# A four-layer transformer chain on one core: context parts packed in their tile, the context laid out by the host, another priority table for the last half

## The chip, the cores and the metric

One NeuronCore of one Trainium2 chip runs the whole program. The metric is the device time of one launch in microseconds (us), lower is better. The engines are TensorE (PE in the profile, with its weight loads apart as PEld), VectorE (DVE), ScalarE (ACT), GpSimd (POOL) and SyncE (SP), which here only issues DMAs (SPq).

## The reference, cut to what matters

16 sequences of 256 tokens by 256 features run through four layers. Each attends to itself, to a context of 77 rows per sequence, or both; 16 heads of 16 features.

```python
# L0: x = LN(x + self_attn(x));  x = LN(x + cross_attn(x, ctx)); x = x + FF(LN(x))      (pre-norm)
# L1: x = LN(x + self_attn(x));  x = LN(x + cross_attn(x, ctx)); x = LN(x + MoE(x))     (8 experts, top 2)
# L2: x = LN(x + self_attn(x, mask)); x = LN(x + cross_attn(x, ctx)); x = LN(x + FF(x))
# L3: x = LN(x + cross_attn(x, ctx))
scores = einsum('bhqd,bhkd->bhqk', q, k) / sqrt(16)
out    = einsum('bhqk,bhkd->bhqd', softmax(scores), v)
```

(The comments stand for the four layer functions; weights, biases and layer-norm gains are inputs. Attentions are numbered 0 to 6 in the kernel: 0, 2 and 4 are self attentions, 1, 3, 5 and 6 are cross attentions with the context.)

## The kernel before, in words

The program has three phases, each a block that all engines run through in an order fixed at build time. Phase a (from 0 to about 1425 us in the trace) takes each of the 16 sequences through layer 0 and the attentions of layer 1 and scatters its tokens by expert. Phase b (to about 1950 us) runs the experts over 39 groups of rows. Phase c, the last half (from about 1950 us to the end at 3045.8 us), gathers the experts' rows and takes each sequence through attention 4 (self, with a mask), 5 (cross), the feed-forward block `l2_ff`, and attention 6 (cross).

**One attention.** TensorE projects the query (`proj`, L714), and ScalarE, VectorE and GpSimd split each projected value into three bf16 parts: `high` (L946, ScalarE), `rest` (L1096, VectorE), `middle` (L951, ScalarE), `low` (L1369, GpSimd). The parts stand in a tile `parts_q` or `parts_k` of [128, 3 parts, 2 halves of the features, 256 tokens]. SyncE copies them by DMA (`copy`, L1430) into a stack, six blocks of 16 partitions each, six DMAs for a stack; a stack then holds [96, 16 heads, tokens], so one bf16 matmul with 96 rows does the product of the split numbers. For the context the tokens are 77: before the change a context part uses 77 of the 256 columns of each half, so every partition gives two runs of 154 bytes. TensorE then makes scores once to find the row maxima (`qm`, L736, with L865 or L869 opening the bank with the mask in self attentions), VectorE reduces them (`max`, L1106), four small VectorE steps split the maxima, TensorE turns them (`turn_shift`, L744), ScalarE copies them (`turned_shift`, L955), and SyncE puts them by DMA into three more rows of the query stack (`shift_in`, L1433). Only then can TensorE make the scores again with the maxima taken off (`km`, L756, with L869 opening the bank in attention 4), ScalarE takes the exponent (L962), and TensorE multiplies by the values (`pv`, L772). VectorE and GpSimd turn and scale the result (L1132, L1136, L1374, L1140), and the output projection (`out`, L802) follows. The feed-forward block is 32 matmuls `ff` (L820, four steps of eight) and 32 of `out` (L802). The context rows of one sequence come by `ctx_load` (L1418), 128 partitions by two runs of 308 bytes in memory; there are 32 of these loads in phase a and 32 in phase c, one for each cross attention of each sequence, and as many context stacks.

**The order of the work.** `Plan.run` is a planner in the kernel's own source. Each step has a duration `us` and a delay `lag` written by hand; the planner walks through a model of the engines and always takes the step that can start first, and of several the one with the highest urgency. The urgency of a step is its remaining way to the end of its sequence in modelled us, divided by 20 (phase a) or 28 (phase c), less the number of its sequence, plus what `ahead_of` reads from the table `AHEAD` for its stage: the entry of the stage and the entry of (stage, attention), added. The stages that matter below: "scores" holds `km` and `exp`, "ffs" `ff` and `relu`, "projs" the projections with their parts and copies, "values" the value projection, "pvs" `pv`, "shifts" the way of the maxima from VectorE to the stack. Up to seven sequences are under way at once (`LANES`). The engines then run their lists in that order and wait on semaphores; nothing is reordered on the chip. For `shift_in` the planner counts 0.76 us and a lag of 2.2 us, times 1.35 for landings in phases a and c:

```python
plan.step("sync", "shift_in", b, at, us=0.76, lag=2.2, after=[("turned_shift", b, at)], gives=["shift"], landing="shift",
over[k], land[k] = end, end + s.lag * (landing if s.landing else 1.0)
urgency = {k: way / per_sequence - self.steps[k].b + (ahead(self.steps[k]) if ahead else 0.0)
plan.run("c", 28.0, ahead_of("c"), 1.35)
```

## Time and profile before

| | us |
|---|---|
| median of 3 runs | 3065.95 (3065.38 to 3067.84) |
| the profiled execution, its own time | 3048.22 |
| its span in the profile | 3045.8 |
| TensorE busy in the span | 2830.4 (93%) |
| VectorE, ScalarE, GpSimd busy | 1681.8, 1331.7, 986.7 |
| packets moved by DMA | 393627, of them 152155 under 512 B |
| mean granted TensorE clock | 0.964 of full |

The page's chain of work that ended last lies on TensorE for 29% of the span and on DMA for 3%, all of it found in phase c (the chain ends at the start of that phase). "Busy" of TensorE is modelled from pipelined matmuls. In the views of waits a line gives the engine and line that waited, what released it, the sum in us, the number of times and the longest one.

### The profile page before, as it was taken

What the parts mean: (1) busy time and instruction counts of PE and PEld (TensorE: products, weight loads), DVE (VectorE), ACT (ScalarE), POOL (GpSimd) and SP (SyncE); (2) the same over time, 40 slices, a digit from 0 to 9 for tenths busy, and PEclk for the clock granted to TensorE, in tenths of its full rate; (3) what the DMA queues carried; (4) which work ended last, traced back from release to release, by engine and by line L of the source; (5) the groups of instructions that cost most, each with busy time, mean ns of one, the idle gap of its engine ahead of it and who ended that gap; (6) DMA issues with size and microseconds to landing.
All of it is one profiled execution on the core that took longest, in us unless ns stands there. A gap on an engine that the chain in (4) does not pass through costs nothing. (4 is left out here: it accounts for less than half of the span.)

```text
span 3045.8 us, 58500 instructions
## 1 busy us (share of the span) xinstructions
PE 2830.4 (93%) x22574; PEld 2279.3 (75%) x22574; DVE 1681.8 (55%) x4086; ACT 1331.7 (44%) x2955; POOL 986.7 (32%) x1103
## 2 busy tenths in 40 slices
PE   6989999989999989975999999889999999999996
PEld 4768888768888777754888888656777777777774
DVE  4646556776755867554110010276676766767664
ACT  2535445556455455332222222245455545555442
POOL 2313224444323444322000000252344444444343
PEclk8999999999999999986999999899999999999997
DMA  9755546585664674754767766375466555666342
GB/s 141 119 72 67 63 54 89 84 114 75 75 71 59 90 98 72 190 74 135 241 225 231 224 211 220 87 111 63 53 85 76 80 79 75 82 77 78 43 50 40
DMA packets 393627, 317.68 MB, mean 104 GB/s; under 512 B 152155, under 2 KB 377307, under 8 KB 393339
## 3 DMA queue, kind: packets, MB, share of 16 engines
q1 hardware_dynamic: 370994, 276.25, 54.6%
q0 software_dynamic: 8272, 23.73, 2.8%
q10 hardware_dynamic: 14085, 13.97, 1.7%
q8 instruction: 179, 2.93, 0.5%
q14 instruction: 97, 0.79, 0.1%
HBM read 133.54 MB, written 36.57 MB: 56 GB/s over the span
## 5 line engine op out<-in xcount | busy, mean ns | idle before, releaser
L962 ACT ACTIVATE a_prob<-a_bank 128x512 f32<-128x512 f32 (+1 forms) x640 | 332.8, 603 | 146.5 <-PE a_bank L756 142.9
L1106 DVE TENSOR_REDUCE a_maxima<-a_bank 128x2 f32<-128x512 f32 (+3 forms) x576 | 339.2, 644 | 82.7 <-PE a_bank L736 82.0
L962 ACT ACTIVATE c_prob<-c_bank 128x512 f32<-128x512 f32 (+1 forms) x512 | 266.3, 599 | 194.7 <-PE c_bank L756 194.4
L989 ACT ACTIVATE b_group_hidden<-b_bank,b_b 128x256 f32<-128x256 f32 (+1 forms) x312 | 123.3, 452 | 387.7 <-PE b_bank L820 387.7
L1106 DVE TENSOR_REDUCE c_maxima<-c_bank 128x6 f32<-128x462 f32 (+1 forms) x448 | 260.4, 635 | 45.2 <-PE c_bank L736 43.9
L865 PE MATMUL a_bank<-a_causal_b,keep_identb 128*128 128x256 bf16 (+1 forms) x768 | 243.1, 316 | 29.9 <-DMA a_qs<-a_shift 12.9
L820 PE MATMUL b_bank<-b_group_xt,b_w 128*128 128x256 f32 (+1 forms) x1248 | 261.6, 364 | 6.3 <-DVE b_group_xt L1157 6.3
L802 PE MATMUL b_bank<-b_w,b_group_hidden 128*128 128x256 f32 x1136 | 251.7, 380 | 0.9 <-ACT b_group_hidden L989 0.9
L820 PEld LDWEIGHTS b_bank<-b_group_xt,b_w 128*128 128x128 f32 x1248 | 220.6, 192 | 33.7 <-DVE b_group_xt L1157 8.3
L802 PEld LDWEIGHTS b_bank<-b_w,b_group_hidden 128*128 128x128 f32 x1136 | 215.6, 190 | 29.7 <-ACT b_group_hidden L989 1.3
L1163 DVE TENSOR_TENSOR b_group_y<-b_bank,b_b 128x512 f32<-128x512 f32 (+1 forms) x39 | 25.1, 644 | 336.1 <-PE b_bank L802 336.1
L1359 POOL TENSOR_TENSOR c_tok<-c_tok,weights_row_L_xattn_ln_g 128x512 f32<-128x512 f32 x64 | 81.2, 1268 | 192.9 <-PE c_bank L705 192.7
L756 PE MATMUL a_bank<-a_qs,a_ks 99*128 99x128 bf16 x1536 | 143.5, 222 | 0.0
L736 PE MATMUL a_bank<-a_ks,a_qs 96*128 96x128 bf16 x1536 | 142.4, 220 | 0.0
L756 PEld LDWEIGHTS a_bank<-a_qs,a_ks 99*128 99x128 bf16 x1536 | 121.6, 99 | 22.9 <-issue 1.4
L736 PEld LDWEIGHTS a_bank<-a_ks,a_qs 96*128 96x128 bf16 x1536 | 120.2, 98 | 23.6 <-issue 2.2
L1132 DVE STREAM_TRANSPOSE a_flat<-a_bank 128x512 f32<-128x512 f32 x128 | 90.0, 708 | 86.5 <-PE a_bank L772 86.0
L714 PE MATMUL a_bank<-a_xt,a_at_q 128*128 128x256 f32 x512 | 131.8, 404 | 5.7 <-ACT a_xt L935 4.4
L802 PE MATMUL a_bank<-a_at_o,a_heads 128*128 128x256 f32 x512 | 131.3, 402 | 5.6 <-DVE a_heads L1140 5.4
L1152 DVE TENSOR_TENSOR a_tok<-a_bank,a_tok 128x512 f32<-128x512 f32 x80 | 54.8, 687 | 146.3 <-PE a_bank L802 146.0
L1369 POOL TENSOR_TENSOR a_parts_q<-a_rest,a_parts_q 128x512 bf16<-128x512 f32 x64 | 74.0, 1158 | 183.0 <-ACT a_parts_q L951 183.0
L1386 POOL DMA_INDIRECT c_pair_y<-sorted_out,keep_rows x64 | 62.8, 982 | 200.7 <-issue 195.1
(255 smaller groups left out, 6224.0 us busy)
## 6 DMA issues: line engine op xcount, KB each, us to landing
b_w<-in_L_xattn_e_w SPq DMA_DIRECT2D x78, 1024.0 KB, 7.4
a_qs<-a_parts_q SPq DMA_DIRECT2D x384, 128.0 KB
c_qs<-c_parts_q SPq DMA_DIRECT2D x288, 128.0 KB
a_ks<-a_parts_k SPq DMA_DIRECT2D x192, 128.0 KB, 5.9
c_ks<-c_parts_k SPq DMA_DIRECT2D x96, 128.0 KB, 5.5
sorted_in<-a_zeros SPq DMA_DIRECT2D x8, 1024.0 KB
b_group_x<-sorted_in SPq DMA_DIRECT2D x32, 256.0 KB, 6.8
sorted_out<-b_group_y ACTq DMA_DIRECT2D x32, 256.0 KB, 4.8
```

The source lines that it names most:

```text
L714: ins = pe.matmul(bank[:, 0, m * n:(m + 1) * n], weight[:, kt, m * P:(m + 1) * P], xt[:, kt, 0:n], start=(kt == 0), stop=(kt == KT - 1))
L736: ins = pe.matmul(bank[:, 0, to:to + m], qs[0:STACK, h, q * P:(q + 1) * P], ks[0:STACK, h, kt * P:kt * P + m], start=(at in CROSS), stop=( ...
L756: ins = pe.matmul(bank[0:kn, 0, to:to + m], ks[0:STACK + NPART, h, kt * P:kt * P + kn], qs[0:STACK + NPART, h, q0:q0 + m], start=(at in CR ...
L802: ins = pe.matmul(bank[:, 0, q * D:(q + 1) * D], heads[:, kt, q * P:(q + 1) * P], weight[:, kt, :], start=(kt == 0), stop=(kt == kts - 1))
L820: ins = pe.matmul(bank[:, 0, j * n:(j + 1) * n], weight[:, kt, f * P:(f + 1) * P], xt[:, kt, 0:n], start=(kt == 0), stop=(kt == KT - 1))
L865: pe.matmul(blocks, k.identb, k.causal[:, keys_first, :].unsqueeze(1).broadcast_to([P, 4 // step, P]), start=True, stop=False)
L962: act.activation(prob[0:rows, first:first + cols], bank[0:rows, 0, 0:cols], ACT.Exp, scale=SCALE).then_inc(k.own(s), 1)
L989: ins = act.activation(hidden[:, f, 0:n], bank[:, 0, j * n:(j + 1) * n], ACT.Gelu, bias=b1[:, f:f + 1])
L1106: v.tensor_reduce(maxima[:, q:q + qn, h:h + n].rearrange("p q h -> p h q"), bank[:, 0, 0:cols].rearrange("p (j q n) -> p j q n", j=n, q=qn ...
L1132: v.transpose(flat, tile(s, "bank")[:, 0, :].rearrange("p (g b c) -> p g b c", g=2, c=32)).then_inc(k.own(s), 1)
L1359: pool.tensor_tensor(x, x, over(k.gains[at][0]), ALU.mult).then_inc(k.own(s), 1)
L1369: pool.tensor_tensor(parts[:, 2, :, 0:n], rest[:, :, 0:n], parts[:, 1, :, 0:n], ALU.subtract).then_inc(k.own(s), 1)
```

## The change

Three edits. (1) `parts_of` gives a context part a packed view of the same tile, so that a part of one partition is one run of 308 bytes (two halves of 77 bf16 values) instead of two of 154; `high`, `rest`, `middle`, `low` and `copy` use it for the context. (2) The host lays the context out as [sequence, partition, half, token], so that `ctx_load` reads one run of 616 bytes a partition instead of two of 308. (3) The table `AHEAD["c"]` is replaced by another one; durations, lags, lanes, buffers and the table for phase a stay. As the modelled durations stay too, the order of phases a and b is what it was.

```diff
--- before.py
+++ after.py
@@ -456,18 +456,16 @@
                ("outs", 2): 152.6, ("norms", 3): 74.0, ("turns", 3): -0.1, ("maxima", 3): 1.6, ("shifts", 3): 0.6,
                ("pvs", 3): 1.3, ("ends", 3): -0.8, ("outs", 3): -0.1, ("norms", "l1_2"): -0.5,
                ("turns", "l1_2"): 0.2, ("gains", "l1_2"): 1.8},
-         "c": {"enters": 2.3, "norms": 8.4, ("norms", 4): -9.6, "turns": 1.2, ("turns", 4): -0.2, "gains": 4.7,
-               ("gains", 4): 30.5, "projs": 0.7, ("projs", 4): -0.5, "values": -0.4, ("values", 4): 1.4,
-               "maxima": -0.2, "shifts": 102.7, ("shifts", 4): 20.1, "scores": 0.2, ("scores", 4): 28.6,
-               "pvs": -0.2, ("pvs", 4): 0.1, "ends": -0.1, ("ends", 4): -48.7, ("enters", 5): 2.2,
-               ("projs", 5): 67.2, ("values", 5): 15.0, "outs": -1.0, ("outs", 4): 0.4, ("norms", 5): -269.4,
-               ("turns", 5): 2.9, ("gains", 5): -88.8, ("maxima", 5): -0.3, ("shifts", 5): 86.2,
-               ("scores", 5): -0.5, ("pvs", 5): 16.5, ("ends", 5): 11.0, ("outs", 5): 9.0, ("norms", "l2_ff"): -4.7,
-               ("turns", "l2_ff"): 18.2, ("gains", "l2_ff"): 5.1, "ffs": 36.7, ("ffs", "l2_ff"): 30.1,
-               ("outs", "l2_ff"): 38.3, ("enters", 6): 1.1, ("projs", 6): 77.4, ("values", 6): 121.8,
-               ("norms", 6): 4.9, ("turns", 6): -1.6, ("gains", 6): 4.8, ("shifts", 6): 2.8, ("scores", 6): 19.9,
-               ("pvs", 6): 129.6, ("ends", 6): -12.2, ("outs", 6): 29.6, ("norms", "l3"): -8.7,
-               ("gains", "l3"): 14.4}}
+         "c": {("ends", 4): 0.8, ("ends", 5): 5.5, ("ends", 6): -1.4, "ends": -1.2, ("enters", "c"): 2.2,
+               ("enters", 6): -1.3, "enters": -0.3, ("ffs", "l2_ff"): 1.9, "ffs": -1.8, ("gains", "l2_ff"): -4.1,
+               ("gains", "l3"): -0.1, ("gains", 4): -8.4, ("gains", 6): -0.4, "gains": 3.0, ("maxima", 5): -0.2,
+               "maxima": -0.2, ("norms", "l2_ff"): 1.3, ("norms", "l3"): 5.6, ("norms", 4): -7.7,
+               ("norms", 5): -16.2, ("norms", 6): -7.2, "norms": 10.8, ("outs", "l2_ff"): 0.1, ("outs", 5): 10.6,
+               ("outs", 6): 1.1, "outs": -0.4, ("projs", 4): -1.5, ("projs", 5): 4.2, ("projs", 6): 13.9,
+               "projs": 1.8, ("pvs", 6): 50.0, "pvs": -0.2, ("scores", 4): 14.9, ("scores", 5): 9.5,
+               ("scores", 6): 2.9, "scores": 4.0, ("shifts", 4): 13.8, ("shifts", 5): 4.5, ("shifts", 6): 1.8,
+               "shifts": 17.5, ("turns", "l2_ff"): 5.3, ("turns", 4): -0.8, ("turns", 6): -1.6, "turns": 1.2,
+               ("values", 4): 1.1, ("values", 5): 6.7, ("values", 6): -0.2, "values": -0.1}}
 
 
 def ahead_of(phase):
@@ -909,6 +907,13 @@
     return qs.rearrange("p h t -> p (h t)").bitcast(F32).rearrange("p (f t) -> p f t", t=S)
 
 
+def parts_of(parts, role):
+
+    if role != "c":
+        return parts
+    return parts.rearrange("p a m t -> p (a m t)")[:, 0:NPART * KT * C].rearrange("p (a m t) -> p a m t", a=NPART, m=KT)
+
+
 def rows_of(sorted_rows, rows):
     return sorted_rows[rows, :].rearrange("(q p) d -> p q d", p=P)
 
@@ -938,7 +943,7 @@
                 ins = act.activation(xt, bank[:, 0, :].rearrange("p (k t) -> p k t", k=KT), ACT.Copy)
             ins.then_inc(k.own(s), 1)
         elif s.kind == "high":
-            bank, parts, n = tile(s, "bank"), tile(s, "parts"), C if s.part == "c" else S
+            bank, parts, n = tile(s, "bank"), parts_of(tile(s, "parts"), s.part), C if s.part == "c" else S
             bias = k.biases[at][0 if s.part == "q" else 1]
             until.wait_ge(*done("proj", b, at, s.part))
             until.wait_ge(*freed(s, "parts"))
@@ -946,7 +951,7 @@
                 ins = act.activation(parts[:, 0, m, 0:n], bank[:, 0, m * n:(m + 1) * n], ACT.Identity, bias=bias[:, m:m + 1])
             ins.then_inc(k.own(s), 1)
         elif s.kind == "middle":
-            parts, rest, n = tile(s, "parts"), tile(s, "rest"), C if s.part == "c" else S
+            parts, rest, n = parts_of(tile(s, "parts"), s.part), tile(s, "rest"), C if s.part == "c" else S
             until.wait_ge(*done("rest", b, at, s.part))
             act.activation(parts[:, 1, :, 0:n], rest[:, :, 0:n], ACT.Copy).then_inc(k.own(s), 1)
         elif s.kind == "turned_shift":
@@ -1088,7 +1093,7 @@
                 ins = v.tensor_scalar(out[:, t, :], x[:, t, :], moments[:, t, 0:1], rstd[:, 1, t:t + 1], ALU.subtract, ALU.mult)
             ins.then_inc(k.own(s), 1)
         elif s.kind == "rest":
-            bank, parts, rest, n = tile(s, "bank"), tile(s, "parts"), tile(s, "rest"), C if s.part == "c" else S
+            bank, parts, rest, n = tile(s, "bank"), parts_of(tile(s, "parts"), s.part), tile(s, "rest"), C if s.part == "c" else S
             bias = k.biases[at][0 if s.part == "q" else 1]
             until.wait_ge(*done("high", b, at, s.part))
             until.wait_ge(*freed(s, "rest"))
@@ -1364,7 +1369,7 @@
                 until.wait_ge(*done("bias_fold", -1, "bias", SHIFT_AFTER[at]))
             pool.tensor_tensor(x, x, over(k.gains[at][1]), ALU.add).then_inc(k.own(s), 1)
         elif s.kind == "low":
-            parts, rest, n = tile(s, "parts"), tile(s, "rest"), C if s.part == "c" else S
+            parts, rest, n = parts_of(tile(s, "parts"), s.part), tile(s, "rest"), C if s.part == "c" else S
             until.wait_ge(*done("middle", b, at, s.part))
             pool.tensor_tensor(parts[:, 2, :, 0:n], rest[:, :, 0:n], parts[:, 1, :, 0:n], ALU.subtract).then_inc(k.own(s), 1)
         elif s.kind == "weigh":
@@ -1415,10 +1420,10 @@
             sp.dma_start(tile(s, "x"), (k.x_in if at == "a" else k.x1)[b]).then_inc(k.own(s), 16)
         elif s.kind == "ctx_load":
             until.wait_ge(*freed(s, "ctx"))
-            sp.dma_start(tile(s, "ctx"), k.ctx_in[b]).then_inc(k.own(s), 16)
+            sp.dma_start(tile(s, "ctx").rearrange("p k t -> p (k t)"), k.ctx_in[b].rearrange("p k t -> p (k t)")).then_inc(k.own(s), 16)
         elif s.kind == "copy":
             role, part = s.part
-            parts, stack, n = tile(s, "parts"), tile(s, "stack"), C if role == "c" else S
+            parts, stack = parts_of(tile(s, "parts"), role), tile(s, "stack")
             if part == 0:
                 until.wait_ge(*done("high", b, at, role))
                 until.wait_ge(*freed(s, "stack"))
@@ -1427,7 +1432,7 @@
             else:
                 until.wait_ge(*done("low", b, at, role))
             for block in COPIES[role == "q"][part]:
-                sp.dma_start(stack[block * HD:(block + 1) * HD, :, :], parts[:, part, :, 0:n]).then_inc(k.own(s), 16)
+                sp.dma_start(stack[block * HD:(block + 1) * HD, :, :], parts[:, part, :, :]).then_inc(k.own(s), 16)
         elif s.kind == "shift_in":
             until.wait_ge(*done("turned_shift", b, at))
             sp.dma_start(tile(s, "qs")[STACK:STACK + NPART, :, :], tile(s, "shift")).then_inc(k.own(s), 16)
@@ -1597,7 +1602,7 @@
     x1 = scratch("x_moe_in", [B, S, D])
     k.x1 = x1.rearrange("b (q p) d -> b p q d", p=P)
     k.out = out.rearrange("b (q p) d -> b p q d", p=P)
-    k.ctx_in = a["ctx_t"].rearrange("(k p) (b t) -> b p k t", p=P, t=C)
+    k.ctx_in = a["ctx_t"]
     k.sorted_in, k.sorted_flat = scratch("sorted_in", [ROWS_SORTED, D]), scratch("sorted_out", [PAIRS * GROUP + SINGLES * HALF, D])
     k.expert_w1 = a["L1_xattn_e_w1"].rearrange("e (k p) n -> e p k n", p=P)
     k.expert_w2 = a["L1_xattn_e_w2"].rearrange("e (k p) n -> e p k n", p=P)
@@ -1755,7 +1760,7 @@
     turn = lambda x: np.moveaxis(x.reshape(x.shape[:-1] + (H // KT, KT, HD)), (-3, -2, -1), (-1, -3, -2)).reshape(x.shape)
     paired = lambda x: np.moveaxis(x.reshape((KT, 2, H // KT // 2, HD) + x.shape[1:]), 1, 2).reshape(x.shape)
     arrays = {"x": v["x"], "mask": v["mask_1x1xSxS_ik0"].reshape(S, S),
-              "ctx_t": v["ctx_1024"].reshape(B * C, D).T,
+              "ctx_t": v["ctx_1024"].reshape(B, C, KT, P).transpose(0, 3, 2, 1),
               "columns": np.concatenate([(turn(v[n].reshape(D)) if n in _TURNED else paired(v[n].reshape(D)) if n in _PAIRED else v[n]).reshape(-1, P)
                                          for n in _VECTORS]).T,
               "rows": np.stack([v[n] for n in ROWS]),
```

## Rows read from the trace of the kernel before

**Rows 1.** The page: busy time, then granted clock in 40 slices.
```profile
PE 2830.4 (93%) x22574; PEld 2279.3 (75%) x22574; DVE 1681.8 (55%) x4086; ACT 1331.7 (44%) x2955; POOL 986.7 (32%) x1103
...
PEclk8999999999999999986999999899999999999997
```

**Rows 2.** Stretches: bounds, length, busy of PE, PEld, DVE, ACT, POOL, clock, DMA, GB/s.
```profile
1950.00:2206.00 256.00, 231.35 (x1641) 166.10 (x1642) 164.42 (x372) 114.69 (x243) 109.55 (x118) 0.93 0.61 84
2206.00:2840.00 634.00, 616.94 (x4928) 469.60 (x4926) 437.50 (x1008) 325.83 (x713) 288.52 (x321) 1.00 0.60 77
2840.00:3045.80 205.80, 176.34 (x1349) 136.96 (x1349) 117.44 (x270) 88.54 (x199) 79.64 (x90) 0.90 0.35 47
200.00:1300.00 1100.00, 1058.47 (x9982) 872.20 (x9983) 725.20 (x1847) 556.30 (x1231) 397.29 (x439) 0.98 0.59 85
```

**Rows 3.** Waits of TensorE from 2206 to 2840 us, the whole list.
```profile
PE c_bank L869 <- DMA c_qs<-c_shift: 17.0, 10, 2.6
```

**Rows 4.** Chain of work that ended last, pieces: start, length, what.
```profile
2310.44 6.95 PE c_bank L820 x32
...
2373.85 6.95 PE c_bank L820 x32
...
2404.56 6.38 DMA c_qs<-c_shift
```

**Rows 5.** Waits of TensorE from 1950 us to the end.
```profile
PE c_bank L869 <- DMA c_qs<-c_shift: 20.9, 13, 3.5
PE c_bank L705 <- DVE c_tok L1088: 11.0, 3, 4.1
...
PE c_bank L756 <- DMA c_qs<-c_shift: 2.0, 2, 1.8
PE c_bank L714 <- DMA c_ctx_t<-in_ctx_t: 1.6, 1, 1.6
```

**Rows 6.** Waits of TensorE in the whole span, those of phase a on DMAs.
```profile
PE a_bank L865 <- DMA a_qs<-a_shift: 12.9, 6, 5.9
...
PE a_bank L865 <- DMA a_qs<-a_parts_q: 10.7, 3, 7.7
...
PE a_bank L756 <- DMA a_qs<-a_shift: 9.4, 6, 3.6
...
PE a_bank L714 <- DMA a_ctx_t<-in_ctx_t: 2.6, 3, 1.9
```

**Rows 7.** DMA in 2437 to 2445 us: queue q1 (packets, MB, share), an issue.
```profile
q1 hardware_dynamic: 1842, 0.43, 33.9%
...
c_ctx_ks<-c_parts_k SPq DMA_DIRECT2D x6, 38.5 KB
```

**Rows 8.** DMA in 2429 to 2437 us, when query copies pass: queue q1.
```profile
q1 hardware_dynamic: 1198, 1.11, 93.4%
```

**Rows 9.** Issues of L1430 by tile: ns min/median/max.
```profile
L1430 SPq DMA_DIRECT2D c_qs<-c_parts_q x288: 551/601/2058, 1974.9 to 2999.1; - x144
...
L1430 SPq DMA_DIRECT2D c_ctx_ks<-c_parts_k x192: 565/617/1870, 1960.8 to 2999.8; - x192
```

**Rows 10.** Groups by line and shape, the two context parts written whole.
```profile
L1369 POOL TENSOR_TENSOR c_parts_k<-c_rest,c_parts_k 128x154 bf16<-128x154 f32 x32 | 15.3, 478 | 38.7 <-ACT c_parts_k L951 38.7
...
L951 ACT ACTIVATE c_parts_k<-c_rest 128x154 bf16<-128x154 f32 x32 | 10.5, 329 | 7.9 <-DVE c_rest L1096 7.9
```

**Rows 11.** Order of time on SyncE's queue, 2463 to 2478 us.
```profile
2468.00 0.76 SPq L1433 DMA_DIRECT2D c_qs<-c_shift  x1
2470.24 3.16 SPq L1430 DMA_DIRECT2D c_qs<-c_parts_q  x3
2473.45 1.94 SPq L1430 DMA_DIRECT2D c_ctx_ks<-c_parts_k  x3
```

**Rows 12.** Order of time on TensorE, 2464 to 2478 us.
```profile
2470.89 1.89 PE L802 MATMUL c_bank<-c_weights_at_o,c_heads 128*128 128x256 f32 x8
2474.12 0.39 PE L869 MATMUL c_bank<-c_weights_mask_k,keep_identb 128*128 128x512 bf16 x1 [1.34 <-DMA c_qs<-c_shift]
```

## The prediction, made before the changed kernel was built or run

> **What bounds the kernel.** The page comes first: TensorE is busy 93% of the span, VectorE 55%, and the clock row shows that TensorE has full clock nearly everywhere but at the start, between the phases and at the end [rows 1]. So only work, idle time or clock of TensorE can move the time. The second view is the table of stretches, because the change touches phase c in one way (its order) and phases a and c in another (the context's bytes). In phase c TensorE's busy time in the three stretches is 231.35 + 616.94 + 176.34 = 1024.6 us of 1095.8, so 71.2 us are idle: 24.7 in the 256 us of the start, 17.1 in the 634 us of the middle, 29.5 in the last 205.8 us [rows 2]. The middle is 97.3% busy. The waits of TensorE there are one single row: 10 waits, 17.0 us together, each for `shift_in` at attention 4 [rows 3]. The chain view says how regular that is: the same feed-forward block comes every 63.4 us (2373.85 - 2310.44), and one DMA of 6.4 us stands in each period [rows 4]. A new order of work must therefore be judged by two things: how many such waits it makes, and what it does to the start and the end, where 54 us of idle time lie and the mean clock is 0.93 and 0.90 [rows 2].
>
> **The context's bytes.** The 384 context copies (four stacks of six in each of 16 sequences) go from 256 packets to 128, 64 loads likewise: 57,344 fewer packets of 393,627. What is a short packet worth? When nearly only context copies pass, 1842 packets take 0.339 x 8 us x 16 engines = 43.4 us, 24 ns each [rows 7]; when query copies pass, 1198 packets of 1 KB take 0.934 x 8 x 16 = 119.6 us, 100 ns each [rows 8]. A context copy is thus 256 x 24 / 16 = 0.38 us of all engines, less than its issue of 0.617 us [rows 9]: SyncE, not the DMA engines, paces such a stack, and the issue of a long-packet copy, 0.601 us, is hardly shorter [rows 9], so I count nothing for the issue. Between a packet price that does not depend on its bytes and one that is all bytes, the saving is 0.19 us or 0 a copy, at most 1.15 us off the queue for a stack. TensorE waits on DMAs after the start are few: the shift and query-copy waits of phase a (6 + 3 + 6 = 15 waits, 33.0 us), three on the context load (2.6 us) [rows 6], and in phase c 15 on the shift (22.9 us) and one on the load (1.6 us) [rows 5]. The ten of the middle have no context copy ahead of them: SyncE issues the shift at 2468.00, and the first context copies come at 2473.45 [rows 11]. That leaves at most 20 waits x 1.15 = 23 us and 4.2 us of load waits, if a stack stood before every one; a context stack is one in three or four, so I take a sixth of it, **-3 us**, with ends 0 and -10.
>
> What the row shows is that a packet of 154 bytes costs 24 ns where one of 1 KB costs 100 [rows 7, 8]. [...]
>
> The engines' own work on a context part (ScalarE 329 ns, GpSimd 478 ns for 128x154 [rows 10]) has the same elements; the parts now start at 154-byte steps. I cost it at nothing: VectorE is 69%, ScalarE 51%, GpSimd 46% busy in the middle of phase c [rows 2], and that idle time hides it. Were each of the 64 context splits 0.3 us slower without cover, it would be 19 us; no row shows a reason.
>
> **The order.** A change of order adds and removes no instruction, so TensorE's 1024.6 us stay but for the clock. The order only decides what stands behind which landing. The wait that exists is a mistake of the model: the planner lets a shift land 0.76 + 2.2 x 1.35 = 3.7 us after its issue, the trace has 2474.12 - 2468.00 = 6.1 us [rows 11, 12], since query and key copies still fill the DMA engines. Whatever order is planned, the 2.4 us error stays; it costs time only where `km` is the next thing on TensorE's list. That is set by the table. Before, `ffs` had 66.8 and the projections of attentions 5 and 6 had 67.9 and 78.1, over `km` with 28.8 (attention 4), -0.3 (5) and 20.1 (6): work of several us is put between a shift and its scores, above all at 5 and 6, and there the middle has no wait at all [rows 3]. Afterwards `km` has 18.9, 13.5 and 6.9, `ffs` 0.1, the projections 6.0 and 15.7. So `km` of 4 and 5 now goes as soon as the model allows, ahead of the 64 matmuls of the feed-forward block that used to cover it. I expect attention 5 to wait as attention 4 does: 1.7 us each (17.0 / 10 [rows 3]). Attention 6 and some of attention 5 keep cover from projections that happen to be ready, so I take 12 further waits of 32 cross attentions: 12 x 1.7 = **+20 us**. The ends are no further wait (or the old ones gone, -21) and all 32 of 1.7 (+54). The start and end I leave as they are.
>
> **Sum.** Against the profiled execution: 3048.2 - 3 + 20 = 3065.2 us. The median of the runs shown is 17.7 us above that execution; the parts are differences and are put on the median: 3065.95 + 17, rounded down to **3082**.
>
> **The rivals.** *Feed-forward as filler, faster.* At lowest rank the feed-forward steps of 1.73 us each (6.95 us for four [rows 4]) are what is left whenever nothing else can start; spread behind the shifts, eight of them could cover the 20.9 us of shift waits in phase c [rows 5]. For it: the waits of the middle need only 1.7 us of cover. Against it: the planner does not know that cover is needed. Price: -21 - 3 = -24: **3042**; it could reach 3025 if the start, where three layer-norm waits cost 11.0 us [rows 5], packs better as well. *Same packing.* TensorE is the bound and any order with seven sequences under way may fill it as well: only the bytes remain, **3063**. For it: phase a, under a table where the feed-forward has low rank, is 96.2% busy from 200 to 1300 us (1058.47 of 1100), 1.1 points below the middle of phase c [rows 2], and it has only 12 shift waits [rows 6]. (By that rate alone phase c would be 12 us longer, between this case and mine.) *Feed-forward pushed to the end, slower by much.* If low rank leaves the blocks of the last three or four sequences until nothing else is left, the last attentions 6 come with no cover: the end's 29.5 us of idle time doubles, and half clock (the stretch has 0.90 of full) adds some 15 (an estimate: today the stretch loses 205.8 x 0.10 = 20 us of clock): +45 - 3, **3108**. It decides if more than two such blocks start after the place of the last of today's. That the change doesn't do what it says: the packed parts surely cut packets; the order surely differs; only the share of each is open.
>
> **Chances.** Waits added (3070 to 3100): 0.34. Filler (3025 to 3058): 0.29. Same packing (3056 to 3069): 0.20. Pushed to the end (3095 to 3130): 0.17. A measurement of this kernel tells about 0.2% from no change, 6 us; so faster, below 3059.8, takes 0.29 and a quarter of the third case, 0.33 together; same takes 0.14 of the third case and the nearest edges of the first and second, 0.19; slower the rest, 0.48. Both signs hold much. The range runs from 3040 to 3112: it leaves out the lower half of the second case and a third of the last. My likeliest case alone is 3070 to 3100.
>
> **What would show it.** Right: the packets drop by about 57,000; phase a, whose order is unchanged, moves by less than 10 us; the waits of TensorE in phase c list L756 behind the shift with ten or more waits near 1.7 us; the span of phase c is some 20 us above 1095.8. Wrong: the sum of shift waits falls under 10 us (filler); or the idle time of the last 200 us grows past 45 us (pushed to the end); or phase a alone gains more than 10 us, which would mean that short packets had held up the shifts.

## The result: faster by 0.84%, where slower by 0.5% was forecast

The changed kernel takes 3043.58 us (median of 7 runs, 3040.6 to 3050.39). The kernel before, run beside it on the same chip, takes 3072.01 us (3065.38 to 3085.62, 7 runs). The ratio is **0.9916, 95% interval [0.9901, 0.9932]**. The forecast was 3082, with a range of 3040 to 3112. Its likeliest case (3070 to 3100) did not happen, and the sign was wrong.

The chips of these runs differ among themselves by nearly as much as the change is worth: the kernel before takes 3050.13 us on the one of e13 to e15 and 3069.08 on the one of e16 to e18, 0.6% more. Timed on another chip, beside a kernel before of 3052.43 us, the changed kernel (run e7 below) takes 3022.63 us: ratio 0.9903 [0.9885, 0.9922]. Spans are therefore compared within one chip, or stretch by stretch. Four single executions of the runs below took two to five times as long as the rest and are left out of the ratios.

The page of the kernel after, beside [rows 1], with the line of its packets:

```profile
PE 2832.3 (93%) x22574; PEld 2279.5 (75%) x22574; DVE 1693.0 (56%) x4086; ACT 1329.9 (44%) x2955; POOL 986.1 (32%) x1103
...
PEclk9989999999999999995999999989999999999997
...
DMA packets 336285, 317.69 MB, mean 104 GB/s; under 512 B 86620, under 2 KB 319964, under 8 KB 335996
```

The same instructions, the same megabytes, 57,342 fewer packets, as counted. The span is 3040.9 us. The profiled execution of the kernel before (3048.22 us) is none of the seven timed beside this one, of which the fastest took 3065.38, so these two profiles may come from different chips; e8 and e7 below are a pair from one chip. The table of stretches, for the places of [rows 2] shifted by 8.2 us since phase b starts that much later in this execution (phase a, to which "Where the packed parts pay" comes back, is longer here and not shorter), with all of phase c behind them, first after and then before (bounds, length, busy of PE, PEld, DVE, ACT, POOL, clock, DMA share, GB/s):

```profile
1958.20:2214.20 256.00, 228.78 (x1647) 165.63 (x1648) 172.53 (x372) 113.64 (x243) 108.48 (x116) 0.94 0.50 83
2214.20:2848.20 634.00, 628.23 (x5009) 479.59 (x5008) 458.74 (x1028) 328.06 (x722) 292.48 (x326) 1.00 0.50 78
2848.20:3040.90 192.70, 163.57 (x1264) 127.43 (x1262) 101.93 (x249) 84.13 (x189) 75.87 (x86) 0.92 0.31 50
...
1958.20:3040.90 1082.70, 1020.58 (x7916) 772.66 (x7916) 733.20 (x1647) 525.84 (x1153) 476.83 (x528) 0.97 0.47 74
```

```profile
1950.00:3045.80 1095.80, 1024.63 (x7916) 772.66 (x7916) 719.36 (x1647) 529.06 (x1153) 477.72 (x528) 0.96 0.56 73
```

Phase c holds the same 7916 matmuls and is 13.1 us shorter. TensorE's idle time fell from 71.2 to 62.1 us; the other 4.0 us are busy time, which goes with a clock of 0.97 in place of 0.96. The idle time is 27.2 us at the start (24.7 before), 5.8 in the middle (17.1) and 29.1 at the end (29.5). So the gain is the middle: the row that filled it before, ten waits for the shift [rows 3], is nearly gone. The waits of TensorE in the middle stretch of the kernel after, the whole list, and then the first of its waits in all of phase c (beside [rows 5]):

```profile
PE c_bank L742 <- DVE c_least_parts L1130: 4.3, 10, 1.4
PE c_bank L867 <- DMA c_qs<-c_shift: 1.1, 5, 0.3
PE c_bank L754 <- ACT c_prob L967: 0.2, 1, 0.2
PE c_bank L800 <- ACT c_prob L967: 0.2, 1, 0.2
```

```profile
PE c_bank L703 <- DVE c_tok L1093: 12.6, 4, 7.7
PE c_bank L800 <- DVE c_heads L1145: 10.3, 7, 3.2
PE c_bank L742 <- DVE c_least_parts L1130: 9.1, 16, 1.7
```

Where a shift is waited for, the order of time on SyncE's queue and on TensorE shows why it costs so little now (beside [rows 11, 12]; in brackets the idle time before the instruction and what ended it):

```profile
2659.03 0.75 SPq L1438 DMA_DIRECT2D c_qs<-c_shift  x1
```

```profile
2659.74 1.99 PE L800 MATMUL c_bank<-c_weights_at_o,c_heads 128*128 128x256 f32 x8
2661.57 0.60 PE L754 MATMUL c_bank<-c_qs,c_ctx_ks 99*77 99x256 bf16 x4
2662.00 0.38 PE L734 MATMUL c_bank<-c_ctx_ks,c_qs 96*128 96x77 bf16 x6
2662.22 1.97 PE L712 MATMUL c_bank<-c_xt,c_weights_at_q 128*128 128x256 f32 x8
2664.12 1.07 PE L770 MATMUL c_bank<-c_prob,c_ctx_values 77*32 77x256 f32 x16
2665.35 0.39 PE L867 MATMUL c_bank<-c_weights_mask_k,keep_identb 128*128 128x512 bf16 x1 [0.16 <-DMA c_qs<-c_shift]
```

The landing is as late as it was, 2665.35 - 2659.03 = 6.3 us (6.1 before [rows 11, 12]), but TensorE has other work nearly up to it: an output projection, scores, a query projection and a value product. It waits 0.16 us instead of 1.34. The feed-forward block is not what stands there: in the chain it still comes whole, 32 matmuls of 6.91 us at a time, every 62.3 us (2380.45 - 2318.12) where it was 63.4 [rows 4]:

```profile
2318.12 6.91 PE c_bank L818 x32
...
2380.45 6.91 PE c_bank L818 x32
...
2442.80 6.91 PE c_bank L818 x32
```

### The profile page after: what moved, and what is told of

Its sections match the earlier page's. It is cut to its first block and busy times, and to the rows that moved or that the text cites. A ratio compares the mean times of both kernels' runs of the same rounds, so it can differ in the third digit from the quotient of the medians.

```text
span 3040.9 us, 58523 instructions
## 1 busy us (share of the span) xinstructions
PE 2832.3 (93%) x22574; PEld 2279.5 (75%) x22574; DVE 1693.0 (56%) x4086; ACT 1329.9 (44%) x2955; POOL 986.1 (32%) x1103
## 5 line engine op out<-in xcount | busy, mean ns | idle before, releaser
L1111 DVE TENSOR_REDUCE c_maxima<-c_bank 128x6 f32<-128x462 f32 (+2 forms) x448 | 262.9, 633 | 39.5 <-PE c_bank L734 39.2
L800 PE MATMUL a_bank<-a_at_o,a_heads 128*128 128x256 f32 x512 | 135.0, 410 | 5.6 <-DVE a_heads L1145 5.5
```

The lines of the kernel that those rows point to most:

```text
L800: ins = pe.matmul(bank[:, 0, q * D:(q + 1) * D], heads[:, kt, q * P:(q + 1) * P], weight[:, kt, :], start=(kt == 0), stop=(kt == kts - 1))
L1111: v.tensor_reduce(maxima[:, q:q + qn, h:h + n].rearrange("p q h -> p h q"), bank[:, 0, 0:cols].rearrange("p (j q n) -> p j q n", j=n, q=qn ...
```

## The experiments

Lengths of stages: a is from the start to the first transposition of phase b, b is 526.1 us long in both kernels, c is the rest. Ratios are to the kernel before on the same chip, with 95% intervals.

| run | what it is | ratio | a | c |
|---|---|---|---|---|
| e8 | kernel before again | 0.9989 [0.9973, 1.0006] | 1434.4 | 1091.9 |
| e7 | kernel after again | 0.9903 [0.9885, 0.9922] | 1417.5 | 1077.8 |
| e1 | packed parts, host-laid context, old table | 0.9927 [0.9911, 0.9942] | 1426.6 | 1088.7 |
| e2 | new table alone | 0.9961 [0.9947, 0.9975] | 1428.7 | 1082.3 |
| e3 | packed parts alone | 0.9942 [0.9927, 0.9956] | 1418.0 | 1084.5 |
| e4 | host-laid context alone | 0.9994 [0.9984, 1.0005] | 1429.5 | 1092.3 |
| e5 | packed parts in phase a alone | 0.9966 [0.9953, 0.998] | 1420.1 | 1092.3 |
| e6 | packed parts in attentions 5 and 6 alone | 0.9979 [0.9967, 0.9991] | 1425.5 | 1086.3 |
| e9 | parts at steps of 78 columns, packets as before | 0.9996 [0.9985, 1.0007] | 1426.1 | 1093.8 |
| e10 | kernel before, planned lag of phase c's shifts 4.0 for 2.2 | 1.057 [1.0546, 1.0594] | 1427.2 | 1270.2 |
| e11 | kernel after, the same | 1.0272 [1.0253, 1.0291] | 1423.4 | 1190.0 |
| e12 | kernel after, 4.0 in phase a too | 1.0546 [1.0526, 1.0565] | 1497.0 | 1188.0 |
| e13 | kernel before, shift issued by ScalarE | 0.9977 [0.9967, 0.9988] | 1426.3 | 1091.0 |
| e14 | e1, shift issued by ScalarE | 0.9934 [0.9915, 0.9952] | 1415.9 | 1077.4 |
| e15 | kernel after, shift issued by ScalarE | 0.9961 [0.9945, 0.9976] | 1420.8 | 1091.0 |
| e16 | kernel before, ten shifts covered by hand | 1.0008 [0.9993, 1.0022] | 1441.5 | 1099.2 |
| e17 | e1, ten shifts covered by hand | 0.9963 [0.9949, 0.9976] | 1431.4 | 1089.8 |
| e18 | kernel before, the same work moved to behind the scores | 1.0031 [1.0017, 1.0045] | 1443.5 | 1104.3 |

### The parts of the change, one at a time (e1 to e4, e7, e8)

e1 has every hunk of the diff but the table; e2 has the table alone. e3 has the packed parts without the host's layout, e4 that layout alone, which is these three edits:

```diff
-            sp.dma_start(tile(s, "ctx"), k.ctx_in[b]).then_inc(k.own(s), 16)
+            sp.dma_start(tile(s, "ctx").rearrange("p k t -> p (k t)"), k.ctx_in[b].rearrange("p k t -> p (k t)")).then_inc(k.own(s), 16)
...
-    k.ctx_in = a["ctx_t"].rearrange("(k p) (b t) -> b p k t", p=P, t=C)
+    k.ctx_in = a["ctx_t"]
...
-              "ctx_t": v["ctx_1024"].reshape(B * C, D).T,
+              "ctx_t": v["ctx_1024"].reshape(B, C, KT, P).transpose(0, 3, 2, 1),
```

> The packed context parts and the host-laid context, with the table for the last half that the kernel before has. Theory O (the order did it: it removes the waits on the shift in phase c): within 0.15% of the kernel before, ratio 0.9985 to 1.0; the wait row of L867 behind the shift stays near 17 to 21 us and the feed-forward block still comes every 63.4 us. Theory B (the bytes did it: short packets had held up the shifts and copies): ratio 0.991 to 0.994, the shift waits under 8 us, a period near 62.3 us. The packets drop by 57,344 under both.

> The other table for the last half, with the layout that the kernel before has. Theory O: ratio 0.991 to 0.993, period of the feed-forward block near 62.3 us, shift waits of phase c under 5 us. Theory B: ratio 0.997 to 1.0, since the new order alone only moves the waits. A third theory, that the two need each other (the new order's cover is just long enough with fewer packets): both single edits give less than a third of 0.84%.

> Only the packed context parts: 49,152 packets fewer, the context loads and the table as before. Theory O: ratio 0.9985 to 1.0005. Theory B: nearly all of what the layout gives, 0.992 to 0.995, because 384 of the 448 transfers that are shortened are these copies.

> Only the context laid out by the host: 8,192 packets fewer, the parts and the table as before. Theory O and theory B: ratio 0.999 to 1.001; the TensorE waits on the context load (2.6 and 1.6 us) may halve. More than 0.2% either way would say that HBM reads of 308 bytes cost far more than their 8,192 packets.

Measured: the layout is worth 0.73%, the table 0.39%; their sum, 1.12%, is 0.15 more than both together in e7, within what the intervals leave open. Of the layout, the packed parts are 0.58% and the host's part nothing that can be told from zero. The layout of the parts is thus the larger half of the gain, about 18 us, and not the 3 of the prediction. It does not come by the waits on the shift in phase c, as the second theory had it: they are 23.0 us in e1, where under 8 was expected. The table gains where +20 us was forecast, less than its own theory had (0.991 to 0.993). In phase c TensorE's waits on the shift come to 4.1 us, against 25.9 in e8:

```profile
PE c_bank L742 <- DVE c_least_parts L1123: 8.7, 15, 1.7
PE c_bank L754 <- DMA c_qs<-c_shift: 4.1, 7, 1.2
```

```profile
PE c_bank L756 <- DMA c_qs<-c_shift: 25.9, 13, 3.8
```

The first fence is e2, the second e8, both waits of TensorE in phase c. Here too the least parts take a piece back: 8.7 us where e8 has 2.8.

> The changed kernel once more, beside the others on one chip. If the two parts add, 0.9927 x 0.9961 = 0.989 (3018 us where the kernel before has 3051). If they share one source (both shorten the wait on the shift in phase c), 0.991 to 0.993.

> The kernel before, word for word, for a trace from this chip: ratio 0.9985 to 1.0015, the start of phase b between 1425 and 1440 us, the sum of TensorE's waits on the shift in phase c 20 to 26 us.

Both repeat what the first pair gave, and give each stage on one chip: phase a 1434.4 against 1417.5 us, phase c 1091.9 against 1077.8.

### Where the packed parts pay (e5, e6)

Both are e3 with the packed view in some attentions only:

```diff
+def parts_of(parts, role, at):
+    if role != "c":
+        return parts
+    if at not in (1, 3):          # e6: (5, 6)
+        return parts[:, :, :, 0:C]
...
```

> The context parts are packed in phase a alone (attentions 1 and 3); phase c, the loads and the table as before. Packing in both phases gave 0.9942. If the gain is spread as the copies are (half of the 384 in each phase), this gives 0.9965 to 0.998 and the start of phase b comes 5 to 10 us earlier than in the kernel before. If only phase c gains (its regular wait on the shift shrinks), this gives 0.999 to 1.001. If only phase a gains, 0.993 to 0.996.

> The context parts are packed in phase c alone (attentions 5 and 6). Spread: 0.9965 to 0.998. Only phase c: 0.993 to 0.996, with less idle time of TensorE between 2206 and 2840 us than 17 us. Only phase a: 0.999 to 1.001, start of phase b as in the kernel before.

Each shortens its own phase and leaves the other. Phase a is 1429.5 us long in the mean of e8, e4, e2 and e6, which have its parts unpacked, and 1420.6 in that of e1, e3, e5 and e7. Lengths scatter with the clock (1434.4 us at 0.95 of full in e8, 1425.5 at 0.96 in e6); TensorE's idle time in it does so less: 134.5 to 135.5 us in the former, 124.1 to 127.2 in the latter. Other executions show less of this. The kernel after of the first pair has 137.1 us of idle time in a phase a of 1436.4, beside 135.0 and 1428.3 in the kernel before. Of e16 to e18, whose hand edits touch phase c alone and which ran on another chip, e16 and e18 have 137.5 and 137.7 us, and e17, with packed parts, 134.6; the ratio of e17 to e16 is 0.9955, where e1 has 0.9927. The gain in phase a thus shows in the time of e5 (0.9966); in the idle time it is 7 to 11 us on the chips of e1 to e8 and 3 on that of e16 to e18, and the first pair, perhaps of two chips, shows none. Phase c is 5.6 us shorter in e6 and 7.4 in e3 than in e8, but 3.2 in e1, of which the slowest of its six executions was profiled (3043.63 us, median 3030.63). No single wait carries it. Phase a of e8, then of e7, in the table of stretches:

```profile
0.00:1434.40 1434.40, 1298.88 (x12129) 1059.03 (x12129) 904.35 (x2348) 678.36 (x1489) 491.63 (x548) 0.95 0.60 88
```

```profile
0.00:1417.50 1417.50, 1293.43 (x12129) 1053.43 (x12129) 903.95 (x2348) 678.32 (x1489) 491.20 (x548) 0.95 0.58 89
```

Idle time is 135.5 against 124.1 us. Some waits of TensorE in those stretches, e8 first (rows left out between them changed less):

```profile
PE a_bank L756 <- DMA a_qs<-a_shift: 9.2, 6, 3.6
...
PE a_bank L865 <- DMA a_qs<-a_parts_q: 8.1, 2, 7.9
...
PE a_bank L865 <- DVE a_maxima L1106: 6.0, 5, 3.4
...
PE a_bank L714 <- DMA a_ctx_t<-in_ctx_t: 3.2, 2, 2.9
```

```profile
PE a_bank L754 <- DMA a_qs<-a_shift: 7.6, 4, 3.4
...
PE a_bank L863 <- DMA a_qs<-a_parts_q: 6.9, 2, 6.6
...
PE a_bank L863 <- DVE a_maxima L1111: 3.1, 5, 1.0
...
PE a_bank L712 <- DMA a_ctx_t<-in_ctx_t: 1.7, 2, 1.4
```

Each gives one to three microseconds, together 7.2 of the 11.4. That the packed parts shorten just these is not shown: in the first pair the same four come to 27.5 us before and 26.7 after. What does land earlier is, first, the context copy itself: the median context copy of phase a takes 3.4 us from its issue to its landing in e8 and 2.6 in e7 (the page's DMA issues; the last column):

```profile
a_ctx_ks<-a_parts_k SPq DMA_DIRECT2D x192, 38.5 KB, 3.4
```

```profile
a_ctx_ks<-a_parts_k SPq DMA_DIRECT2D x192, 38.5 KB, 2.6
```

The context load does so too in e3, where it is not changed itself: 4.5 us against 5.8 in phase a, 2.7 against 3.9 in phase c. The key copies don't (5.8 and 5.9 us in phase a, 5.5 in both in phase c), nor do the shifts for which TensorE waits in phase c (6.4 us in both). So some transfers beside the packed ones gain and some do not; by which of them the time reaches TensorE stays open.

### Is it the number of packets, or the place of the bytes? (e9)

```diff
-    return parts...[:, 0:NPART * KT * C].rearrange("p (a m t) -> p a m t", a=NPART, m=KT)
+    return parts...[:, 0:NPART * KT * (C + 1)].rearrange("p (a m t) -> p a m t", a=NPART, m=KT)[:, :, :, 0:C]
```

e3 with one column left free behind each run of 77: the parts stand as close as in e3, but the two halves no longer touch.

> The context parts lie nearly packed: the second half begins after 78 columns, not 77, so a copy keeps its 256 packets of 154 bytes, while everything else (where ScalarE, VectorE and GpSimd write, how far apart the runs lie) is as in the packed kernel, with the table and loads of before. If the number of packets is what counts: ratio 0.9985 to 1.001, the context copy's median time to landing stays near 3.4 us, the start of phase b near 1430 us. If the engines or the density count: 0.993 to 0.996, as with packed parts, and 1418 us.

Nothing that can be told from zero is left of e3's 0.58% (idle time of phase a: 132.4 us, 2 to 3 less than in the other four): 393,627 packets as in the kernel before, a ratio of 0.9996, and 3.5 us to the landing. So the gain is the count of packets (or, which this cannot part, the length of each run), and neither where the parts lie nor what the engines do to them. What the packets cost is seen in e4 and e1, one chip and the packed parts as the only difference, from q1's share of 16 engines' time over the span: 54.0% of 3047.9 us in e4, 51.2% of 3041.4 in e1.

```profile
q1 hardware_dynamic: 362802, 276.25, 54.0%
```

```profile
q1 hardware_dynamic: 313650, 276.25, 51.2%
```

That is 26,334 - 24,915 = 1419 us of engine time for 49,152 packets fewer, 29 ns each. The trace holds the size and time of every packet and says where it comes from. 98,304 packets of 154 bytes took 24.0 ns in the mean in e4, 49,152 of 308 bytes took 31.9 in e1: a pair becomes a third cheaper, 796 us in all, 0.13 us of all engines for a copy. Most of the rest, 505 us, is the 206,848 packets of 1 KB, whose mean went from 100.2 to 97.8 ns though nothing about them was changed.

### Is the table's gain the cover of the shift? (e10 to e18)

The planner lets a shift land 3.7 us after its issue; one at attention 4 took 6.1 [rows 11, 12]. e10 to e12 let the planner count 6.2 for every shift:

```diff
-    plan.step("sync", "shift_in", b, at, us=0.76, lag=2.2, ...
+    plan.step("sync", "shift_in", b, at, us=0.76, lag=4.0 if at in (4, 5, 6) else 2.2, ...
```

(These are the shifts of phase c; e12 has 4.0 everywhere.)

> The kernel before with one number of the planner put right in phase c: the lag of the shift's landing 4.0 instead of 2.2, so that it counts 0.76 + 4.0 x 1.35 = 6.2 us as the trace shows. If the new table's gain is that it covers this landing, this order loses most of the 19 to 21 us of shift waits too: ratio 0.995 to 0.998 and waits on the shift in phase c under 8 us. If cover is not what matters, or another wait takes its place: 0.999 or above.

> The changed kernel with the same lag of 4.0 in phase c. It has 2.3 us of shift waits left in the middle, so there is little to take: 0.989 to 0.992 against the kernel before (the changed kernel alone 0.990). Above 0.994 would say that the table fits only the lags it was made with.

> The changed kernel with the lag of 4.0 in phases a and c. Phase a still waits 20.6 us on the shift in 11 places; if the planner covers half of them the ratio is 0.986 to 0.989 and phase b starts near 1410 us. If its table was fitted to the lag of 2.2, phase a gets longer and the ratio is above 0.992.

All three are 3 to 6% slower (e12 has 80 us more in phase a than e7, 1497.0 against 1417.5). In e10 the waits on the shift do fall, from 25.9 to 6.6 us, but others rise far more. The first of its waits in phase c:

```profile
PE c_bank L744 <- DVE c_least_parts L1125: 41.0, 15, 5.7
PE c_bank L705 <- DVE c_tok L1088: 26.5, 12, 4.5
PE c_bank L802 <- DVE c_heads L1140: 25.1, 12, 4.5
PE c_bank L736 <- DMA c_qs<-c_parts_q: 14.6, 9, 4.1
```

These runs say nothing on cover. Nor had they made the model truer. The trace holds the semaphore increments of each DMA, four for a shift; put to the issues in their order, they give its landing. In e8, 34 of the 48 shifts of phase c land within 3.7 us (median 2.9). In the middle stretch the ten of attention 4 take 5.7 to 8.2 us, and the twenty of attentions 5 and 6 take 2.7 to 3.0. The one at attention 4 stands behind twelve copies of 128 KB, issued in the 10 us before it (from 2400.16 us on for the shift at 2410.31). So the planner's 3.7 us were wrong for one attention in three, and e10 to e12 made them wrong for the other two. A lag of 4.0 at attention 4 alone was not tried, so that a table's ranks hold only for the durations they were found with is not shown.

e13 to e15 leave the order alone and send the shift over ScalarE's queue, where no query or key copy stands in front of it:

```diff
+            shift_in = k.plan.steps["shift_in", b, at, 0]
+            until.wait_ge(*done("turned_shift", b, at))
+            act.dma_start(tile(shift_in, "qs")[STACK:STACK + NPART, :, :], tile(s, "shift")).then_inc(k.own(shift_in), 16)
...
-            sp.dma_start(tile(s, "qs")[STACK:STACK + NPART, :, :], tile(s, "shift")).then_inc(k.own(s), 16)
+            pass
```

> The kernel before with the DMA of the maxima (shift_in) issued by ScalarE on its own DMA queue, right after it has copied them, so that it does not stand behind the query and key copies in SyncE's queue; the planner's order is untouched. If the queue is why a shift lands after 6.1 us and not after 3.7, TensorE's waits on the shift fall from 25.9 + 22.2 us to under 10, ratio 0.985 to 0.993. If the landing is slow for another reason: 0.998 or above.

> The same with the packed context and the host-laid context, but the old table: the layout's 0.9927 and the last one's gain added, if the packets cost time by their own landing; if the layout gained only because shifts waited behind context packets, no better than the last kernel.

> The changed kernel with the shift on ScalarE's queue; it differs from the last kernel by the table alone. If the new table gains by covering the shift's landing, the table is now worth less than a third of its 10 us: within 0.1% of the last kernel. If it gains by something else (fewer small gaps, a faster first maxima step), still 0.3 to 0.4% better than the last kernel, about 0.980 to 0.984 against the kernel before, and the fastest of all.

The landing at attention 4 stayed as late, 6.4 us in e13 (2401.47 to 2407.89) and 6.7 in e15 (2654.47 to 2661.20), so it is not SyncE's queue that makes it late. The waits on the shift became 18.1 us in e13, which gains 0.23%, between its two expected ranges (0.985 to 0.993, or 0.998 and above), and 14.8 in e14, whose ratio is that of e1; in e15 they rose to 9.7, and the table's advantage was gone: 0.9961 against 0.9934 of e14. In phase a of all three a single wait of 15 us for a query copy came up, which hides part of what the queue gives. The first waits of e15 in phase c:

```profile
PE c_bank L800 <- DVE c_heads L1148: 10.2, 7, 3.1
PE c_bank L867 <- DMA c_qs<-c_shift: 9.7, 10, 2.9
PE c_bank L742 <- DVE c_least_parts L1133: 8.9, 16, 1.7
PE c_bank L712 <- ACT c_xt L940: 7.9, 12, 1.7
```

In e15 ScalarE has an issue more than the new order was planned with, and its `c_xt` is waited for twelve times, 7.9 us (twice, 2.8 us, in e7). That this is why the table's advantage is gone was not tested by itself.

The last three edit TensorE's list by hand under the old table. A value projection of the next sequence (8 matmuls, 1.9 us) is pulled some 15 steps forward, in ten sequences: to in front of the scores that wait for the shift (e16; e17 on the layout of e1), or, as a control, to behind their first four (e18). ScalarE's copy out of that bank moves with it, ahead of the exponentials, and the banks are dealt out anew in TensorE's order. These three ran on a chip where the kernel before takes 3069.08 us.

```diff
+def cover(plan, phase, at=4):
...
+    for b in range(4, 15):
+        i = next(j for j, s in enumerate(tensor) if key(s) == ("km", b, at, (0, 0)))
+        j = next((j for j in range(i, min(i + 25, len(tensor))) if tensor[j].kind == "value_proj"), None)
+        if j is None or tensor[j].at != at:
+            continue
+        tensor.insert(i, tensor.pop(j))          # e18: i + 4
+        x = tensor[i]
+        m = next(n for n, s in enumerate(scalar) if key(s) == ("exp", b, at, (0, 0)))     # e18: (1, 0)
+        n = next(n for n, s in enumerate(scalar) if key(s) == ("value", x.b, x.at, 0))
+        if n > m:
+            scalar.insert(m, scalar.pop(n))
...
+        cover(plan, "c")
```

> The kernel before with its old table, but the planned list of TensorE is edited behind the planner: at ten sequences (5 to 14) the value projection of the next sequence (8 matmuls, 0.236 us each, 1.9 us) is taken from its place some 15 steps later and put right in front of the first key-query products of attention 4, which wait for the shift. Nothing else changes. Theory 'the new table's gain is cover': the ten waits of 1.9 us in the middle of phase c (18.9 us in the kernel before) fall under 6 us and do not come back elsewhere; phase c becomes 8 to 14 us shorter, ratio to the kernel before 0.994 to 0.9975. Rival 'the gain is the packing of the planner as a whole': the shift waits go, but waits for other producers take their place (as with the larger planned lag), phase c within 4 us of 1091.9, ratio 0.9985 to 1.001.

> The same edit of TensorE's list on the packed parts and host-laid context with the old table. 'Cover': 0.987 to 0.9905 (the layout's 0.9927 and 8 to 14 us less), phase c 1075 to 1081. 'Packing': 0.9915 to 0.9935, phase c 1084 to 1089.

> Control: the same value projections are pulled forward, but to behind the first four key-query products of attention 4 instead of in front of them. 'Cover': the ten waits of 1.9 us on the shift stay as they are (16 to 20 us), phase c within 3 us of 1091.9, ratio 0.9985 to 1.001. 'Pulling the value projection forward helps by itself': phase c shorter as in the kernel with the cover in front, ratio under 0.998.

Some waits of TensorE in phase c, first e16, then e18 (the row of `c_tok`, 13.5 and 13.0 us against 10.6 in e8, is left out above both):

```profile
...
PE c_bank L769 <- DVE c_least_parts L1150: 12.2, 13, 1.9
...
PE c_bank L894 <- ACT c_prob L987: 9.0, 12, 1.4
PE c_bank L894 <- DMA c_qs<-c_shift: 5.6, 5, 3.7
...
PE c_bank L781 <- DMA c_qs<-c_shift: 2.3, 2, 1.9
```

```profile
PE c_bank L894 <- DMA c_qs<-c_shift: 21.1, 13, 3.5
...
PE c_bank L769 <- DVE c_least_parts L1150: 12.1, 13, 1.9
```

e16 takes the waits on the shift from 25.9 us (e8) to 7.9, and gains nothing: ten new waits on the least parts cost 12.2 - 2.8 = 9.4 us, and twelve on the exponentials 9.0, since ScalarE now has the value's bank in front of them. e18 shows the first of these alone: shift waits as before (23.2 us), least parts again 12.1, 0.31% slower, which is 9.5 us of 3069, and outside both of its expected ranges. The likeliest reading is that the value projection, where it stood, had covered the chain of the maxima (`least_parts`) of the next attention. A part may be something else: the four small VectorE steps of that chain take 1770 ns together in e16 and 1516 in e8, which over 13 waits is up to 3 us. e17 has the same three, 12.1, 9.0 and 5.5 us, and at 0.9963 lies 0.36% above e1's 0.9927 (from another chip), in neither of its ranges. "Cover" as I had put it, ten waits that go and nothing else, is refuted: here the fill was already in use. The rival, packing as a whole, fits the waits but has no test of its own: the kernel after has both, 1.1 us of waits on the shift and 9.1 on the least parts, 10.2 together, where the kernel before has 22.9 + 2.8 = 25.7 [rows 5 for the shift] and e16 12.2 + 9.0 + 7.9 = 29.1. What in the new ranks makes that possible was not separated.

## Why the prediction was wrong

**What bounds the kernel** held: TensorE is 93% busy in both, and the gain is idle time of it, in phase c 9.1 of 13.1 us.

**The context's bytes** failed on size: -3 us was taken, with ends 0 and -10, and the packed parts alone give -0.58% [0.44, 0.73] of 3051, some 18 us; with the host's layout 22. The price of the packets was in its bounds: 0.13 us of all engines for a copy, between 0 and 0.19; a packet of 308 bytes takes 31.9 ns in e1, 1.3 times the 24.0 ns of one of 154 in e4. (A sixth of 23 us is 3.8 and not 3, which changes nothing.) The step that failed is the next one, that such a saving reaches TensorE only through the waits on shifts, query copies and context loads, and only where a context stack stood right ahead. With it the issue on SyncE was taken to hide the rest (0.617 and 0.601 us; 0.617 and 0.598 came out). In its place the runs show landings that move by more than the price of the packets: 0.8 us for the context copies of phase a, 1.2 to 1.3 for the context loads, and 2.4% less time for a 1 KB packet in the mean (100.2 to 97.8 ns). That TensorE's idle time, spread over many small waits, shrinks by them is argued and not shown wait by wait; that it is the packets is shown by e9.

"Phase a moves by less than 10 us" came out in the first pair, though in the other direction (8.1 us longer), and between the means (8.9), and failed in e7 against e8 (17 us). The text had named more than 10 us as the sign that short packets hold up the shifts. The shifts that TensorE waits for in phase c land no earlier, and the waits on the shift in phase a fell by 1.6 us only (22.2 to 20.6), so it is not by them.

**The engines' work on the parts** at nothing: right. ScalarE's whole part takes 332 ns (329 [rows 10]), GpSimd's 479 (478).

**The order** failed on its sign: +20 us was expected, and the table gives -0.39% [0.25, 0.53], 12 us, with a phase c 9.6 us shorter in e2 than in e8. The step that failed is that `km`, once ahead of the block that used to cover it, makes attention 5 wait as attention 4 does. It has two faults. The late landing that it counts on is not there: the 6.1 us were read at attention 4, and in the middle stretch the shifts of attentions 5 and 6 land after 2.7 to 3.0 us, within what the planner allows. And the ranks were read in pairs, as if the feed-forward block were the only cover: an output projection, a query projection and a value product stand there (the list of 2659 to 2665 us), and the waits at attention 4, where the landing is late, went as well, from 17.0 to 1.1 us. What in the new table brings that work there, the runs do not show.

**Start and end unchanged**: right for the end (29.1 against 29.5 us idle), 2.5 us too little for the start.

**The rivals.** *Filler* (0.29, 3042) came nearest: its number was off by 1.6 us and its sign of the sum of shift waits, under 10 us, is there. But its mechanism was not what happened: the feed-forward still comes in whole blocks, and of its -24 us only 12 are the order's, the rest being packets. *Same packing*, 3063, is refuted by e2. *Pushed to the end* is refuted by the idle time of the end. The range held the time by 3.6 us; put on the median of 3065.95 it was given for, the ratio makes 3040.2, its very edge. That it lies inside is luck: both errors have one sign, -15 us for the bytes and -32 for the order, and the range, 42 us below the forecast, had room for the second alone. (At its other end it leaves out half of the last case, 3112 to 3130 of 3095 to 3130, and not a third.)

## What to carry to other kernels

Count packets as well as bytes and issues. Here, with the DMA engines 0.5 to 0.6 busy, making two runs of 154 bytes into one of 308 was worth six times what the waits listed before it suggested, and left the issue as long as it was. Look at a landing for each kind of transfer before you call a model's number wrong: one late kind in three looked like all of them, and both the forecast and e10 to e12 were built on it. Do not judge a planner's new ranks by comparing two of them; what else is ready at that time counts too. And before filling one wait with work from elsewhere, ask what that work covered where it stood: e18 gives the price of that alone, 0.31%.

## What the hardware showed that I had not expected

A small VectorE instruction of the same form differs by its surroundings: the one on 128x32 elements at the head of the least parts takes 743 ns in phase c of the kernel before and 300 after (288 and 248 in phase a). The groups of VectorE by line and shape, before, then after:

```profile
L1112 DVE TENSOR_SCALAR c_least_parts<-c_maxima 128x32 bf16<-128x32 f32 x48 | 35.7, 743 | 1.7
```

```profile
L1117 DVE TENSOR_SCALAR c_least_parts<-c_maxima 128x32 bf16<-128x32 f32 x48 | 14.4, 300 | 1.7
```

With the new table alone (e2) it is 282 ns, with the layout alone (e1) 746; so it goes with the order of work. The traces settle what it goes with: GpSimd. Where no GpSimd instruction overlaps it, it takes 181 ns in the mean and at most 182, in e8 as in e7 (8 and 16 of the 48). The others are counted by the instruction that overlaps them longest. Beside a `TENSOR_TENSOR` of GpSimd on `c_tok`, `c_parts_q` or `c_normed` it takes 859 to 964 ns in the mean in e8 (39 of the 48), and in e7 only twelve of the 48 have one of these three beside them, at 345 to 518 ns; nine have `c_parts_k` (316 ns), ten `c_rstd` (182 ns). What the small step gained the layer norm's scaling lost, the `TENSOR_SCALAR` of 128x256 elements on `c_tok`: 408 ns alone in e7, 1314 beside GpSimd's `c_tok` (22 of 160, against 3 in e8). Its sum in phase c went from 66.2 to 87.5 us, just what the small step saved. VectorE's busy time there grew by 13.8 us all the same, from 719.4 to 733.2, most of it in two others: the next step of the same chain (`c_least_rest`, 14.3 to 21.6 us) and a sum with `c_pair_y` (15.5 to 21.3).

The shift, 24 KB, lands 2.7 to 3.0 us after its issue in the middle of phase c, and 5.7 to 8.2 behind the query and key copies of attention 4 (e8); issued from ScalarE's queue it takes 5.8 to 9.0 there (e13). And the same program differs between two chips by 0.6% (medians 3069.08 and 3050.13 us, of 27 and 17 executions), three quarters of the whole change.
